# Ternary weights in two VectorE passes instead of three, in an attention and BitNet feed-forward layer on eight cores

## The reference

```python
def weight_quant(w):
    scale = 1.0 / jnp.clip(jnp.mean(jnp.abs(w)), 1e-05)
    return jnp.clip(jnp.round(w * scale), -1, 1) / scale
...
x = x + attention(layernorm(x), W_query, W_key, W_value)    # 8 x 2048 x 1024, 16 heads, causal
x = x + bit_linear(silu(conv3(bit_linear(layernorm(x), w1))), w2)   # 1024 -> 4096 -> 1024
```

## Time and profile before

| | us |
|---|---|
| time before, median of 3 runs (lowest, highest) | 997.62 (995.47, 999.28) |
| the profiled execution, its own time | 999.49 |
| its span, first to last instruction of the slowest core (core 2) | 997.9 |
| spans of the other cores | 988.5 to 995.8 |
| VectorE busy, slowest core | 736.0 |
| ScalarE busy, slowest core | 703.9 |
| TensorE busy, slowest core | 897.3 |

### The profile page before, as it was taken

The page is one execution under the profiler, slowest core; times in us unless marked ns, Lnnn a source line. Parts: engine busy times, 40 slices in busy tenths (PEclk is TensorE's granted clock), DMA queues, the critical chain, the costliest instruction groups (busy, mean ns, idle before and its releaser), DMA issues.

```text
span 997.9 us, 24185 instructions; the slowest of 8 cores (988.5 to 997.9 us)
## 1 busy us (share of the span) xinstructions
PE 897.3 (90%) x7516; PEld 539.9 (54%) x7516; DVE 736.0 (74%) x1202; ACT 703.9 (71%) x1114; POOL 617.4 (62%) x816
## 2 busy tenths in 40 slices
PE   1999899999898889887977679999999999999998
PEld 0454454545454545444655556666666666666443
DVE  2677656666687778767479888989989897877651
ACT  3554798988887878868898867776777777666300
POOL 2220648575654655533365997979889797978650
PEclk9999999999998999989899889999999999999999
DMA  8942666665777668675297321434242333332121
GB/s 263 336 145 90 228 226 214 219 215 202 227 230 222 215 221 231 209 249 199 94 342 249 119 65 65 168 113 164 107 149 85 106 107 124 110 127 87 43 85 43
DMA packets 38893, 166.95 MB, mean 167 GB/s; under 512 B 4977, under 2 KB 5106, under 8 KB 30066
## 3 DMA queue, kind: packets, MB, share of 16 engines
q1 hardware_dynamic: 34354, 148.62, 45.1%
q0 software_dynamic: 4416, 16.78, 4.8%
HBM read 140.22 MB, written 25.17 MB: 166 GB/s over the span
## 4 chain that ended last, share of the span: by engine, by line
PE 68%; DVE 11%; issue 7%; ACT 7%; DMA 5%; POOL 1%; SPq 0%; DVEq 0%; ACTq 0%; POOLq 0%
PE psO L940 21%; PE psM L922 18%; PE psQK L724 7%; PE psS L782 6%; PE psV L699 5%; PE psPV L810 5%; ACT PT L1086 3%; DVE t1s L1305 2%; DMA wbuf<-w2p 2%; DVE t1s L1308 2%; DMA wvst<-wv 2%; DMA wbuf<-w1q 2%; DVE psD L1511 1%; ACT hs L1139 1%; ACT tb L1143 1%
## 5 line engine op out<-in xcount | busy, mean ns | idle before, releaser
L1086 ACT ACTIVATE PT<-psS,nbias 128x1024 bf16<-128x1024 f32 (+1 forms) x320 | 300.5, 986 | 60.7 <-PE psS L782 35.0
L922 PE MATMUL psM<-xqT,w1b 128*128 128x258 bf16 x2048 | 241.1, 276 | 18.0 <-DVE hs L1492 15.9
L646 POOL TENSOR_TENSOR hs<-hs,tb 128x256 f32<-128x256 f32 x256 | 194.5, 784 | 63.8 <-DVE hs L1492 54.2
L922 PEld LDWEIGHTS psM<-xqT,w1b 128*128 128x128 fp8e4 x2048 | 199.3, 98 | 58.8 <-issue 23.0
L1139 ACT ACTIVATE hs<-psM,convb_s,convw_s 128x256 f32<-128x256 f32 x256 | 148.0, 578 | 82.6 <-PE psM L922 57.2
L655 POOL TENSOR_TENSOR hs<-hs,srow 128x256 f32<-128x256 f32 x240 | 178.8, 779 | 17.4 <-ACT srow L1157 17.4
L1492 DVE SCALAR_TENSOR_TENSOR hs<-psM,convw_s,hs 128x256 f32<-128x256 f32 x256 | 114.6, 475 | 21.8 <-ACT tb L1143 20.9
L724 PE MATMUL psQK<-ln1T,wqkb 128*128 128x512 bf16 x480 | 125.7, 386 | 1.7 <-DVE qkE L1229 0.5
L810 PEld LDWEIGHTS psPV<-vaug,PT 128*128 128x128 bf16 x2176 | 93.3, 99 | 59.8 <-issue 35.2
L1143 ACT ACTIVATE tb<-psM,convw_s 128x256 f32<-128x256 f32 x256 | 123.8, 484 | 0.0
L1511 DVE TENSOR_REDUCE psD<-hs 128x256 f32<-128x1024 f32 x56 | 109.3, 1952 | 18.8 <-ACT hs L1150 18.8
(11 more groups left out here) (146 smaller groups left out, 1088.3 us busy)
## 6 DMA issues: line engine op xcount, KB each, us to landing
wbuf<-w1q SPq DMA_DIRECT2D x32, 1024.0 KB, 6.9
wbuf<-w2p SPq DMA_DIRECT2D x32, 1024.0 KB, 6.8
w1b<-t1scr SPq DMA_DIRECT2D x64, 512.0 KB, 3.5
x<-x SPq DMA_DIRECT2D x16, 512.0 KB, 15.2
wqkst<-wqk POOLq DMA_DIRECT2D x16, 512.0 KB, 8.1
x1scr<-x POOLq DMA_DIRECT2D x4, 2048.0 KB, 9.1
x1g<-x1scr SPq DMA_DIRECT2D x16, 512.0 KB, 4.3
out<-x1g SPq DMA_DIRECT2D x16, 512.0 KB, 3.0
```

The lines of the kernel that those rows point to most:

```text
L646: e.tensor_tensor(hs_quad(q)[:, part], hs_quad(q)[:, part], tb_quad(q)[:, part], ALU.add).then_inc(g_add, 1)
L922: inst = e.matmul(psM[j][:, 0:GRP + 2], w1b[:, at:at + 128], xqT[:, x0:x0 + GRP + 2], start=(kc == 0), stop=(kc == 7))
L1086: e.activation(out=pt_unit(u).rearrange("p (h w) -> p h w", w=512)[:, :, 128 * j:512], in_=psS[u % 2][:].rearrange("p (h w) -> p h w", w=512)[
```

## The change

The float16 tile t1s becomes an int16 tile of the same size. The first pass multiplies by the scale and takes the maximum with -1; the conversion to int16 on the way out does the rounding. The second pass takes the minimum with 1 and writes fp8. The pass that did both bounds is gone, and so is one wait for VectorE's own write.

```diff
-        t1s = sb("t1s", [128, 2048], F16, esA)
+        t1s = sb("t1s", [128, 2048], I16, esA)
...
-                done(e.tensor_scalar(t1s[:], wsl, smalls[:, scol:scol + 1], 1536.0,
-                                     ALU.mult, ALU.add))
-                settled()
-                done(e.tensor_scalar(t1s[:], t1s[:], 1535.0, 1537.0, ALU.max,
-                                     ALU.min))
+
+                done(e.tensor_scalar(t1s[:], wsl, smalls[:, scol:scol + 1], -1.0,
+                                     ALU.mult, ALU.max))
                 settled()
                 if i >= 2:
                     e.wait_ge(d_wo[i % 2], 16 * (i // 2))
-                e.tensor_scalar(t8s_slot(i), t1s[:], -1536.0, None, ALU.add,
-                                saturate=False).then_inc(v_ws, 1)
+                e.tensor_scalar(t8s_slot(i), t1s[:], 1.0, None,
+                                ALU.min, saturate=False).then_inc(v_ws, 1)
```

More of the change, by code:

```diff
@@ L11 @@
 F8 = mybir.dt.float8e4
+I16 = mybir.dt.int16
 AF = mybir.ActivationFunctionType
```

## The result

| | before | after |
|---|---|---|
| median of the runs, us | 997.35 | 986.50 |
| lowest to highest, us | 995.47 to 999.28 (4 runs) | 984.45 to 987.36 (4 runs) |
| the profiled execution, us | 999.49 | 984.45 |
| its span, slowest core, us | 997.9 (core 2) | 982.9 (cores 4 and 6) |

The ratio is 0.9889, 95% interval 0.9871 to 0.9908: 1.1% faster, 0.1 us from the forecast of 986.6. The two profiled executions differ by 15.0 us, because before's was one of its longer ones and after's its shortest; the medians differ by 10.9.

The account below looks back on a forecast made before the run. VectorE's queue, holding up scores and nbias in head pairs 3 to 6, was taken as the bound. 17 x 0.87 = 14.8 us, three quarters kept (11), gave 988.5 profiled, 986.6 median; forecast 980 to 992, range 978 to 998.

Parts of the forecast that it names:

- The sign that the prediction named for it: In ScalarE's exponentials (L1086), the wait for nbias would be gone or under 2 us.
- the sum: 32 x 0.87 = 27.8 us of VectorE work removed; 14.8 on core 2's chain, 11 us taken over cores.
- all of it arrives: Rival: the 17 chain steps save 1.10 each, stalls included, plus head pair 7 and steadier clock; about 977 us; chance 0.07.
- The saving of 0.87 a step: In each ternary weight step, removing L1308 and its wait saves 0.87 us start to start; step 3.54 to 2.67.
- The rivals in which one or both passes slow to 2.28: Weight-step passes at the slower rate: one slow, 1000 us, chance 0.04; both slow, 1017 to 1033 us, chance 0.06.
- The removed pass: Prediction's paragraph on L1308: counts 0.87 us a step; GpSimd stalls move to the last pass; 1.10 if they went.
- The rival in which the transfers give the gain back: In head pairs 3 to 6, loads slow as steps follow closer; about 4 us gained, 994 us; chance 0.13.
- over 8 us in the middle: Weight loads landing in over 8 us, against 7.8, would speak for transfers giving the gain back.
- The limit of 45.8 us for a head pair: Core 4's head pair 3, shortest with masks and ternary steps; four are 183.2, 15.0 below core 2's 198.2.
- The four times 43.6 us: Head pair 1's time as baseline for head pairs 3 to 6: 174.4 against 198.2, so 23.8 us lost on core 2.
- Head pair 7 was to give 1 to 1.7 us: Head pair 7 has two weight steps, priced at 1 to 1.7 us in all.
- three quarters of 14.8: Of 14.8 us (17 chain steps of core 2 at 0.87), 11 us was taken for the maximum over cores.

Follow-up runs that it names:

- three_int16: Kernel after with one int16-to-int16 pass put back between its two passes; 998.16 us, ratio 1.0016 against the kernel before.
- half: Kernel after with the middle pass put back for w2 only, so two passes for w1, three for w2; 992.24 us, ratio 0.9938 against before.
- four_int16: Kernel after with two int16-to-int16 passes put back, one pass more than before; 1010.72 us, ratio 1.0139 against before.
- adds_after: Kernel after, GpSimd's residual additions of head pairs 3 to 6 held until the weight step behind the division has ended; 984.34 us, ratio 0.9858 against before.
- early_load: Kernel after, with the load released behind the first of two passes and issued ahead of the store; 984.25 us, ratio 0.9862 against before.
- before_early: Kernel before, three passes kept, with the load released behind the first pass and issued ahead of the store; 992.60 us, ratio 0.9945 against before.
- one_pass: Kernel after cut to one float32-to-fp8 pass, without whole-number rounding and upper bound; 979.40 us, ratio 0.9824 against before.

## Why the prediction was right

**The mechanism.** VectorE's in-order queue holds the copies of Q, the divisions and nbias behind the weight steps, and part of every pass in it was on the chain. Three runs show this: three_int16 brings the old time back, half gives a little over half, in the head pairs where the pass is gone, and four_int16 costs about what the change gave. The sign that the prediction named for it came nearly as named: ScalarE's wait for nbias, 5.4 us on core 2 before, is 2.0 us on core 6 after.

**What the sum left out: the clock.** The sum has no term for TensorE's clock; a steadier clock stands only in the case "all of it arrives". The second table shows that it was a large part of the way in which the queue cost time. Before, TensorE ran at 0.50 for 9.8 us of head pairs 3 to 6 in the mean of eight cores, in 21 stretches, each of them behind a pause of TensorE of 1.0 to 2.3 us; after, for 2.1 us, in three stretches on three cores. Here is one on core 2 of before, from the order in time: a stalled pass, ScalarE's wait for the nbias behind it, TensorE's pause for ScalarE, then the windows around the pause and of the stretch itself.

```profile
297.17 3.27 DVE L1308 TENSOR_SCALAR t1s<-t1s 128x2048 f16<-128x2048 f16 x1
...
302.12 4.13 ACT L1086 ACTIVATE PT<-psS,nbias 128x1024 bf16<-128x1024 f32 x4 [2.69 <-DVE nbias L1269]
...
303.38 0.39 PE L782 MATMUL psS<-qkE 64*128 64x512 bf16 x2 [2.12 <-ACT PT L1086]
...
300.00:305.60 5.60, 3.01 (x25) 1.31 (x23) 3.85 (x10) 3.48 (x4) 1.24 (x2) 1.00 0.70 217
305.60:312.50 6.90, 6.90 (x50) 3.75 (x48) 6.20 (x9) 4.13 (x5) 6.41 (x6) 0.51 0.59 189
```

TensorE was busy through all of this stretch, so at half the clock about half of it is lost. If that holds for all of them, the clock accounts for some (9.8 less 2.1)/2 = 3.8 of the 8.7 us gained in head pairs 3 to 6 and (12.8 less 7.7)/2 = 2.6 of the 3.2 in head pair 7. This is an estimate, and an upper one, since TensorE isn't busy throughout in every such stretch. No run holds the clock apart from the waits that precede its falls: as far as the rows show, the same late work costs once as a wait and again as a slow stretch.

**The passes.** Both were priced nearly right: 1.28 and 1.29 forecast, 1.27 and 1.23 undisturbed (shortest), an integer on one side included. The 1.29 of the earlier trace rows wasn't quite undisturbed: before, too, the last pass took 1.23 in the median. The saving of 0.87 a step holds within 0.05: 3.49 less 2.67 is 0.82 between the shortest steps, 3.92 less 3.01 is 0.91 between the means, which hold the stalls. The rivals in which one or both passes slow to 2.28 are out. What the Trainium skill says in "VectorE: DVE Perf Modes" ("What auto-detection actually checks"), that size and place of the operands decide, agrees with these durations and with the int16 pass of three_int16.

**The stalls with GpSimd live on.** Said under "The removed pass", and seen: 3.74 us for a last pass of 1.23, 2.5 us over, as 3.29 was 2.5 over 0.76. Had they gone, a step would have saved 1.10; it saved 0.91 in the mean. In the kernel after on core 6 the last pass of that slot began at 340.06, and GpSimd's four additions and a square ran from 340.03 to 342.71:

```profile
338.61 1.28 DVE L1307 TENSOR_SCALAR t1s<-wbuf,smalls 128x2048 int16<-128x2048 f32 x1
340.06 3.73 DVE L1312 TENSOR_SCALAR t8s<-t1s 128x2048 fp8e4<-128x2048 int16 x1 [0.17 <-DVE t1s L1307]
...
340.03 1.69 POOL L543 TENSOR_TENSOR x<-x,ctx 128x128 f32<-128x128 f32 x4
341.68 1.03 POOL L523 TENSOR_TENSOR sqb<-qkE 128x512 bf16<-128x512 bf16 x1
```

adds_after took them away, so it was right not to count them as saved, and the case "all of it arrives" didn't come. What the Trainium skill says in "SBUF — State Buffer" ("Who interferes with whom"), that one of the two blocks for the whole instruction of the other, agrees with this; that VectorE stayed out over five GpSimd instructions in a row is what these rows add. Which of the two came first the rows don't tell: by the recorded starts the pass is 0.03 us behind the additions here and 0.04 ahead of them in the earlier trace rows, and GpSimd's starts are rough.

**The load.** The rival in which the transfers give the gain back is out: they moved 226 to 248 GB/s in head pairs 3 to 6 after the change, and from issue to landing a load took 6.9 and 7.0 us there (w1 and w2, median, core 6), for 7.0 and 6.8 before (core 2). So its sign, over 8 us in the middle, didn't come. Its kernel of truth is the waits: they grew to 18.7 us, and early_load got some 2.7 us or less by removing most of them. What the prediction didn't foresee is that an earlier load alone, with all three passes kept, reaches half of the change's gain (before_early). The two gains overlap: the same edit gives 5.5 us from before and 2.7 from after.

**Terms that were mis-sized**, though they cancelled. The limit of 45.8 us for a head pair was too high: head pair 3 took 44.7 on core 6, and one_pass put the floor at 44.8 to 45.0. The four times 43.6 us against which the loss of 23.8 was counted were too low, since head pair 1 has no masks on TensorE; 198.2 less one_pass's 179.9 is 18.3. Core 4 was to come from 190.3 to 183.2 in head pairs 3 to 6. It came to 187.3, 3.0 us for 7, since its head pair 4 took 50.4. Head pair 7 was to give 1 to 1.7 us and gave 5.5 on core 4 (55.8 to 50.3) and 3.4 on core 2 (56.0 to 52.6), 3.2 in the mean of eight cores. The prediction priced its two steps, and not what waits behind the first of them. On core 2 of before that step starts at 439.73, as soon as its load has landed; the division and, behind it, the scores follow, and ScalarE had waited 5.85 us for them. On core 6 of after the same wait is 1.72, the last line here:

```profile
432.44 7.12 DMA wbuf<-w2p
439.73 1.30 DVE t1s L1305
...
447.21 3.44 ACT L1086 ACTIVATE PT<-psS,nbias 128x1024 bf16<-128x1024 f32 x3 [5.85 <-PE psS L782]
...
430.80 3.12 ACT L1087 ACTIVATE PT<-psS,nbias 128x1024 bf16<-128x1024 f32 x3 [1.72 <-PE psS L783]
```

The earlier load alone brings head pair 7 down as far (before_early, 51.6 us). The step "three quarters of 14.8" was a judgement over the cores, 11 us; the medians give 10.9. That closeness is partly luck: head pairs 3 to 6 gave 8.7 in the mean, head pair 7 the rest, and part of both came by the clock, for which there was no term.

**Head pair 4.** The forecast was 46 to 47 us. On six cores it took 45.9 to 47.2; on cores 2 and 4, 50.1 and 50.4. The difference of some 3 us is the clock: on these two alone it fell to 0.50 in this head pair, for 6.8 us. Core 2's chain holds a projection of four matmuls at either level, and a window of core 4 shows the lower one:

```profile
294.47 0.97 PE psQK L725 x4
...
298.87 1.81 PE psQK L725 x4
...
302.00:306.00 4.00, 4.00 (x27) 2.40 (x26) 3.15 (x7) 2.23 (x2) 4.00 (x5) 0.50 0.66 223
```

Shortly before, TensorE had stood still for 1.26 us on core 2 and 1.87 us on core 4. But cores 0, 3, 5, 6 and 7 stood still for 1.22 to 1.27 us at the same place and kept the full clock. Why these two and not the others stays open. Core 6 had the only fall of the clock in head pair 6, which took 47.6 us there and 45.1 to 45.2 on the others.

## What to carry to other kernels

An engine that is busy three quarters of the time can still be on the chain through its queue: compare stretches with and without the suspected work (50 us here, against 45 once nearly all of it is gone) and price the edit per step, start to start. Look at the clock of the stretches too: where late work makes TensorE pause, a slow stretch can follow, and the gain of an edit that removes the pause holds both. Then look at what else the freed instruction was waiting for, since a stall with another engine can move to the next instruction and not leave with the one removed, as here. When a buffer is free after the first of several passes, tell the loader then: on three passes that alone was worth half as much as removing a pass.

## What the runs showed of the hardware

An int16 tile runs at the float16 rates in all three forms tried: float32 to int16 in 1.27 us, int16 to int16 in 0.69 (shortest; 0.76 in the median), int16 to fp8 in 1.23, for 2048 columns. A VectorE pass of this kind that met four GpSimd additions waited for all four and for the square behind them, 2.5 us, without getting in between. TensorE's granted clock fell from 1.00 to 0.50 behind pauses of 1.0 to 2.3 us in head pairs 3 to 6 (21 times on the eight cores of before), but pauses of 1.22 to 1.27 us passed without a fall on five cores of after.
